# First query step moved beside the last key tiles, and the start of the next pair's attention reordered, in a convolution, attention and routed-MLP kernel

## What is computed

```python
x = x + conv(_gn(x), ...)      # x: (16, 64, 56, 56) f32; conv below
t = to_tokens(x)               # 3136 tokens of 64 features for each image
t = t + attention(_ln_t(t))    # 16 heads of 64, features elu + 1, linear attention
t = t + routed_mlp(_ln_t(t))   # 32 experts, each takes its 8 best tokens
x = from_tokens(t)

# conv: t3[a,k,b] = sum over pixels of x shifted by 2k-6 columns times x
#       t12 = 5x5 dilated depthwise(x) - (7-tap product with t3 - 1x5 depthwise(t2)), t2 = 1x3 conv(x)
# attention: q, k = elu(proj) + 1; positions enter as cos and sin
qkv   = q_cos @ (k_cos.T @ v) + q_sin @ (k_sin.T @ v)
denom = 1 / (q_cos . sum(k_cos) + q_sin . sum(k_sin) + 1e-5)
out   = (qkv * denom) @ dense_w.T + dense_b
```

## Time and profile before

| | |
|---|---|
| median of 3 runs | 3526.32 us (3520.82 to 3526.87) |
| the profiled execution: time, span | 3529.31 us, 3527.5 us |
| PE busy in the span | 3191.5 us (90%) |
| DVE, ACT, POOL busy | 2415.9, 1975.6, 1968.3 us |
| granted TensorE clock, mean | 0.982 |
| one pair in the loop | about 415 us |

### The profile page before, as it was taken

The page is one execution under the profiler, slowest core; times in us unless marked ns, Lnnn a source line. Parts: engine busy times, 40 slices in busy tenths (PEclk is TensorE's granted clock), DMA queues, the critical chain, the costliest instruction groups (busy, mean ns, idle before and its releaser), DMA issues.

```text
span 3527.5 us, 44913 instructions
## 1 busy us (share of the span) xinstructions
PE 3191.5 (90%) x17092; PEld 1488.6 (42%) x17092; DVE 2415.9 (68%) x2773; ACT 1975.6 (56%) x2209; POOL 1968.3 (56%) x1303
## 2 busy tenths in 40 slices
PE   3898999989899998989989898998989999899977
PEld 2543345434443335433454344443354333543333
DVE  5887766967668676776668666686756866645754
ACT  1166654766556764666646665476645676444430
POOL 1167861878428882478727785297833888121320
PEclk8999999999999999999999999999999999999988
DMA  2002740046300661016510363005620075202678
GB/s 55 19 1 57 156 104 28 1 98 146 82 19 0 145 143 56 1 29 152 133 31 0 80 152 85 28 1 125 141 60 19 2 161 135 52 1 65 149 169 279
DMA packets 69297, 278.75 MB, mean 79 GB/s; under 512 B 30845, under 2 KB 35485, under 8 KB 64221
## 3 DMA queue, kind: packets, MB, share of 16 engines
q1 hardware_dynamic: 69085, 275.89, 32.5%
HBM read 242.78 MB, written 33.05 MB: 78 GB/s over the span
## 4 chain that ended last, share of the span: by engine, by line
PE 72%; DVE 11%; ACT 7%; DMA 5%; issue 4%; SPq 1%; POOL 0%; DVEq 0%; ACTq 0%; POOLq 0%
PE ps_D L1590 15%; PE ps_C L1523 10%; PE ps_A L1508 5%; PE ps_B L1508 5%; PE ps_D L1523 5%; PE ps_E L1568 5%; PE ps_E L1523 5%; PE ps_B L1552 3%; PE ps_D L1366 3%; PE ps_A L1552 3%; DVE region L1149 2%; PE ps_A L1385 2%; DMA RB<-r_keep 2%; DVE arena L1000 2%; DMA r_keep<-RR 2%
## 5 line engine op out<-in xcount | busy, mean ns | idle before, releaser
L610 POOL TENSOR_TENSOR arena<-arena,UHL 128x896 f32<-128x896 f32 x525 | 1106.6, 2112 | 252.8 <-ACT UHL L771 252.6
L1590 PE MATMUL ps_D<-region,small 128*128 128x448 f32 x1792 | 759.3, 550 | 9.7 <-DVE OS L1185 6.6
L592 POOL TENSOR_TENSOR region<-region,RB 128x896 f32<-128x896 f32 x224 | 468.9, 2093 | 174.9 <-DMA RB<-r_keep 174.5
L771 ACT ACTIVATE UHL<-arena,W8C 128x896 f32<-128x896 f32 x525 | 540.9, 1033 | 0.4
L620 POOL TENSOR_TENSOR UA<-region,CS 128x128 f32<-128x128 f32 (+1 forms) x400 | 224.6, 563 | 449.4 <-PE ps_C L1523 401.3
L1590 PEld LDWEIGHTS ps_D<-region,small 128*128 128x128 f32 x1792 | 322.9, 190 | 291.8 <-issue 237.8
L815 ACT ACTIVATE EQ<-ps_B,NEG 128x896 f32<-128x896 f32 x224 | 225.5, 1007 | 361.4 <-PE ps_B L1552 361.4
L1523 PE MATMUL ps_C<-region,UA 128*128 128x512 f32 (+1 forms) x800 | 382.5, 601 | 18.1 <-ACT region L689 18.1
L1000 DVE SCALAR_TENSOR_TENSOR arena<-arena,W8C 128x448 f32<-128x448 f32 (+1 forms) x235 | 358.3, 1545 | 0.0
L1158 DVE TENSOR_TENSOR region<-region,ps_C 128x896 f32<-128x896 f32 x224 | 242.9, 1084 | 142.3 <-ACT ps_C L779 142.0
L1125 DVE SCALAR_TENSOR_TENSOR region<-region,ps_A 128x1024 f32<-128x1024 f32 (+1 forms) x200 | 242.6, 1213 | 140.2 <-ACT region L797 140.2
(11 more groups left out here) (308 smaller groups left out, 4983.8 us busy)
## 6 DMA issues: line engine op xcount, KB each, us to landing
RB<-r_keep SPq DMA_DIRECT2D x448, 448.0 KB, 6.0
arena<-x SPq DMA_DIRECT2D x8, 1568.0 KB, 6.6
t_keep<-Y SPq DMA_DIRECT2D x7, 1568.0 KB, 5.2
r_keep<-RR SPq DMA_DIRECT2D x448, 7.0 KB, 2.9
w_keep<-region SPq DMA_DIRECT2D x7, 784.0 KB, 5.5
arena<-w_keep SPq DMA_DIRECT2D x4, 784.0 KB, 10.6
arena<-L_ffn_weight SPq DMA_DIRECT2D x1, 2080.0 KB
CST<-cst SPq DMA_DIRECT2D x1, 1568.0 KB, 6.4
```

What stands on the lines that cost most here:

```text
L592: pool.tensor_tensor(out=q, in0=q, in1=RB[:, cc].rearrange("p (c n) -> p c n", c=2), op=ALU.mult).then_inc(pool_scaled.sem, 1)
L610: pool.tensor_tensor(out=X[:, cut], in0=X[:, cut], in1=PRODUCT[m % 3], op=ALU.add).then_inc(pool_taps.sem, 1)
L771: act.activation(PRODUCT[m % 3].rearrange("p (h w) -> p h w", w=W), g_window(2 * g * ROWS + 2 * (k // 5), 2 * (k % 5) - 4, 2 * ROWS), ACT. ...
L1590: ins = pe.matmul(here.area(key)[:, 0:PIX], MW[i][:, c, :], Q[s % 3][:, c, :], start=c == 0, stop=c == NCHUNK - 1)
```

## The change

It renumbers the work around two seams of a pair.

At the seam of key tiles and query slots, step 0 of the queries leaves the slots. The first image's head matrices stand beside key tiles 29 and 31, its four projections beside tiles 33, 35, 37 and 39, its denominators beside 41 and its sums beside 43, all through ps_C, one at a time. Its features lie in un2 and SQ (`features`). DVE's pieces leave tiles 30, 32, ... 42 and 43 (`NO_PIECE`), so that 23 of the 25 are done beside the tiles, up to the last one, and two in slots 12 and 15. The first projection of step 1 stands before the last key product. The slots begin with step 1 and are 66 in number; the second image's head matrices stand in slots 1 and 3, the four outputs of step 0 in slots 2, 4, 6 and 8. Chunks 0 and 2 of step 0 are multiplied by DVE straight from RB in SBUF (`first_scale`), without ACT's copy to PSUM. Tap products fill four of five slots, before three of four.

At the seam of back and key tiles, the turned correlation waits for its copy only (`t3_copied`), `conv(0)` for the turned taps only from its fifth tap, the routing weights are turned before `conv(2)` into ps_A, ps_D and ps_E, group 0 is split before group 1 is turned, and `conv(3)` is last. Group 1 is scaled beside tile 0 and split beside tile 2, and POOL's deviations of group 1 stand before its first UA. Group 3 goes through ps_D beside tile 2.

```diff
-YT_TILES = [None, None, 0, 1]
-SUM_TILES = [None, None, 1, 2]
+YT_TILES, YT_AREAS = [None, None, 0, 2], "__CD"
+SUM_TILES = [None, None, 1, 3]
-SCALE_TILES = [None, None, 8, 12]
-SPLIT_TILES = [None, 0, 9, 13]
-UTS_TILES = [None, 2, 12, 18]
+SCALE_TILES = [None, 0, 8, 12]
+SPLIT_TILES = [None, 2, 9, 13]
+UTS_TILES = [None, 4, 12, 18]
+WT_GROUPS = [(0, 16), (16, 8), (24, 1)]
-PRODUCT_TILE, PRODUCT_SLOT, POOL_LAG, DRAIN_SLOT = 20, 3, 4, 64
+HEAD_TILES, FIRST_TILES, FIRST_DEN, FIRST_SUM = (29, 31), (33, 35, 37, 39), 41, 43
+NO_PIECE = (30, 32, 34, 36, 38, 40, 42, 43)
+PRODUCT_TILE, PRODUCT_SLOT, POOL_LAG, PIECE_SLOT, DRAIN_SLOT = 20, 1, 1, 12, 60
-PRODUCT_SLOTS = {PRODUCT_SLOT + n + n // 3: n for n in range(POOL_PIECES - TILE_PRODUCTS)}
-SLOTS = 4 * STEPS
+PRODUCT_SLOTS = {PRODUCT_SLOT + n + n // 4: n for n in range(POOL_PIECES - TILE_PRODUCTS)}
+SLOTS = 4 * (STEPS - 1)
+HEAD_SLOTS = (1, 3)
+FIRST_OUT_SLOTS = {2: 0, 4: 1, 6: 2, 8: 3}
+FIRST_POOL_SLOTS, FIRST_PARTS_SLOT = {0: 1, 2: 3}, 10
-ALL_SLOTS = 70
+ALL_SLOTS = 66
...
+                uses += [(("m", 0, HEAD_TILES.index(k)), "C")] if k in HEAD_TILES else []
+                uses += [(("qp", 0, FIRST_TILES.index(k)), "C")] if k in FIRST_TILES else []
+                uses += [(("den", 0), "C")] if k == FIRST_DEN else []
+                uses += [(("dsum", 0), "C")] if k == FIRST_SUM else []
...
+            def first_scale(here, cc):
+                q = features(0, cc)
+                dve.wait_ge(*spread_loaded[cc // 2].at(here.pair, 1))
+                dve.tensor_tensor(out=q, in0=q, in1=RB[:, cc].rearrange("p (c n) -> p c n", c=2),
+                                  op=ALU.mult).then_inc(first_scaled.sem, 1)
...
                 norm_sums(squared(0), ln1_sums, 0)
                 norm1_scale(here, pair, 0)
-                norm_sums(squared(1), ln1_sums, 1)
                 low_part(pair, 0)
                 conv_residual(here, pair, 2)
-                norm1_scale(here, pair, 1)
+                norm_sums(squared(1), ln1_sums, 1)
                 conv_residual(here, pair, 3)
...
-                    if conv and k > NORM_TILE:
-                        depthwise(here, pair + 1, K_PIECES, DVE_PIECES)
-                for i in range(2):
-                    head_matrices(here, i)
+                    if k - 1 in HEAD_TILES:
+                        head_matrices(here, 0, HEAD_TILES.index(k - 1))
+                    if k - 1 in FIRST_TILES:
+                        q_features(here, 0, FIRST_TILES.index(k - 1))
+                    if k == FIRST_DEN + 1:
+                        den_parts(here, 0)
+                    if k == FIRST_SUM:
+                        den_guard(here, 0)
+                        den_reciprocal(here, 0)
+                    if conv and k > NORM_TILE and k not in NO_PIECE:
+                        depthwise(here, pair + 1, 1, DVE_PIECES)
+                first_scale(here, 0)
...
             def turned_correlations(here):
-                pe.wait_ge(*here.emptied("t3"))
+                pe.wait_ge(*(t3_copied.first(1) if here.span == "setup" else t3_copied.at(here.pair, 1)))
...
                 turned_correlations(here)
                 conv(here, 0)
                 conv(here, 1)
-                for g in (0, 1):
-                    pe.wait_ge(*here.emptied(("conv", g)))
-                    to_tokens(here, 1, g)
-                    if g == 0:
-                        conv(here, 2)
+                pe.wait_ge(*here.emptied(("conv", 0)))
+                to_tokens(here, 1, 0)
                 routing_weights(here)
+                conv(here, 2)
                 pool_tokens(here)
+                split_tokens(here, pair, 0)
+                pe.wait_ge(*here.emptied(("conv", 1)))
+                to_tokens(here, 1, 1)
+                pool_turned(here)
                 conv(here, 3)
-                pool_turned(here)
-                split_tokens(here, pair, 0)
```

More of the change, by code:

```diff
@@ L95, in slot_of_step, with step_of, chunk_of @@
 def slot_of_step(j, lag):
-    return j >= lag and (j - lag) % 4 == 0 and (j - lag) // 4 < STEPS
+    return j >= lag and (j - lag) % 4 == 0 and (j - lag) // 4 < STEPS - 1
+def step_of(j):
+    return j // 4 + 1
+def chunk_of(j):
+    return j // 4 + 1, j % 4
 def copied_slot(j):
@@ L270, in pair_uses @@
             uses += [(("lg", g), misc()) for g in range(NG)]
-            return uses + ([(("wt", g), misc()) for g in range(2)] + [("pool", "D"), ("pool_turned", "E")] if last
+            return uses + ([(("wt", g), "ADE"[g]) for g in range(3)] + [("pool", "D"), ("pool_turned", "E")] if last
                            else back_uses())
@@ L676, in tokens @@
                     act.wait_ge(*square_free)
+                if which == 2 and g == 0:
+                    act.wait_ge(*here.filled(("out", 0)))
                 src = here.area(key)[:, 0:m * P].rearrange("p (t c) -> p t c", c=P)
@@ L789, in products_out, with q_exponential @@
                         .then_inc(*here.empty(key))
+            def q_exponential(here, s, cc):
+                key = ("qp", s, cc)
+                act.wait_ge(*here.filled(key))
+                act.activation(EQ[:, cc % 2], here.area(key)[:, :].rearrange("p (c n) -> p c n", c=2)[:, :, 0:PIX],
+                               ACT.Exp, bias=NEG1[:, 0:1]).then_inc(eq_ready.sem, 1)
             def pair_of_images(here):
@@ L1145, in q_features @@
                 dve.wait_ge(*eq_ready.at(here.pair, n + 1))
-                if s >= 3:
+                if s == 1 and cc == 0:
+                    dve.wait_ge(*ua_ready.at(here.pair, KTILES))
+                if s >= 4:
                     dve.wait_ge(*(here.filled(("out", s - 3)) if cc == 3
@@ L1262, in _ @@
                 now[0] = lambda n: vstep.at(pair, n)
-                pair_of_images(Here("loop", pair))
+                pair_of_images(Here("loop", pair), Here("loop", pair - 1) if pair else start)
                 assert links[0] == VLOOP, links[0]
@@ L1266, in _ @@
             now[0] = lambda n: vstep.at(PAIRS - 1, n)
-            pair_of_images(Here("last", PAIRS - 1))
+            pair_of_images(Here("last", PAIRS - 1), Here("loop", PAIRS - 2))
             end = Here("final")
@@ L1402, in conv @@
                 if g == 0:
-                    pe.wait_ge(*here.emptied("t3t"))
+                    pe.wait_ge(*here.emptied("t3"))
                     for w in here.all_emptied([("t2", m) for m in range(NG)]):
@@ L1406, in conv @@
                 for k in range(7):
+                    if g == 0 and k == 4:
+                        pe.wait_ge(*here.emptied("t3t"))
                     ins = quarters(here, g, L10[:, k, :],
@@ L1587, in q_output @@
                 pe.wait_ge(*(scaled_by_pool(here.pair, s, cc) if cc in POOL_SCALED
-                             else here.emptied(("rb", s, cc))))
+                             else here.emptied(("rb", s, cc)) if s else first_scaled.at(here.pair, cc // 2 + 1)))
                 for c in (2 * cc, 2 * cc + 1):
-                    ins = pe.matmul(here.area(key)[:, 0:PIX], MW[i][:, c, :], Q[s % 3][:, c, :],
+                    ins = pe.matmul(here.area(key)[:, 0:PIX], MW[i][:, c, :], features(s, cc)[:, c % 2, :],
                                     start=c == 0, stop=c == NCHUNK - 1)
@@ L1618, in pair_of_images @@
                         k_products(here, k - 2)
+                    if k == FIRST_DEN:
+                        for g in range(2):
+                            q_denominators(here, 0, g)
                     if k in UTS_TILES:
@@ L1732, in _ @@
                         .then_inc(*end.fill(key))
-VSETUP = 44
-VLOOP = 12
+VSETUP = 42
+VLOOP = 11
 LOW = -3.0e38
```

237 lines of the change are left out of this document (132 added, 105 removed).

## The result

| | median | lowest to highest | runs |
|---|---|---|---|
| before | 3526.60 us | 3520.82 to 3534.48 | 4 |
| after | 3484.81 us | 3483.41 to 3488.96 | 4 |

The ratio is 0.9882, 95% interval 0.9861 to 0.9903: the change makes the kernel faster by 42 us, half of the 83.5 that were forecast, and the time lies above the range of 3405 to 3480. The profiled execution has a span of 3487.2 us at a mean granted clock of 0.975.

What follows compares the result with a forecast made beforehand. PE was taken to bound the kernel, with only its idle 30 us a pair to win. First seam 28 plus second seam 55.5 made 83.5 us off 3529.3, 3445.8, about 3443 as median; 80% range 3405 to 3480.

Steps and rivals of the forecast that it cites:

- What bounds the kernel, and where the idle lies: PE is busy 384.7 of 415 us a pair; of its idle, 10.9 us lie at the first seam, 8.6 at the second.
- Second seam, 55.5 us: From correlation's end to the fourth key product: idle nearly all gone, 7.5 us in seven pairs and 3 in the first.
- the 0.8 kept back: Second seam: 0.8 us a pair taken off the walked 8.3 us, for hops between engines.
- The 3 us of the first pair: Second seam of the first pair: 3 us won, since its first tiles show the same two waits.
- Key tiles, 11.0 us: First seam: key tiles end about 11.0 us later, 7.8 work moved in, 6.1 waits, 0.7 hops, less 3.4 slack.
- The rival that all seven hand-overs cost 2.6 us: Key tiles: every ps_C hand-over costs 2.6 us, 18.2 us of waits instead of 6.1; slower than before, 3540; 4%.
- Slots, "comes to the first output of step 1 27.4 us after": Query slots: first output of step 1 comes 27.4 us after the end of the key tiles, by walking both queues.
- the price of `first_scale` at 1.95 us: Start of the slots: each DVE multiplication from RB takes 1.95 us, the 1949 ns row measured where POOL runs.
- the gain of 15.0: Slots: first output of step 1 comes 27.4 instead of 42.4 us after the key tiles, winning 15.0 us a pair.
- first seam gives nothing: Rival: new waits at the ps_C hand-overs use up the first seam's 28 us; 3471 us; 13%.
- What the changed profile would show: PE busy nearly unchanged, span 75 to 90 us shorter, `first_scale` 1.6 to 2.1 us, ps_C waits of 2.6 and 0.8.
- The three signs named for a wrong forecast: ps_C waits above 2 us each, DVE's first slots late for RB, or the first key product waiting for POOL.

Runs made afterwards that it cites:

- s2: The kernel before with only the second-seam part of the change, query step 0 left in the slots; 3459.94 us, ratio to before 0.9802.
- e1: The changed kernel with POOL's two scalings of step 0 moved from slots 0 and 2 to slots 3 and 5; 3432.80 us, ratio to before 0.9724.
- e2: The changed kernel without DVE's piece behind key tile 49, made up later; 3472.89 us, ratio to before 0.9837.
- e3: The changed kernel with the two `first_scale` operations beside key tiles 48 and 49, in place of the pieces there; 3483.66 us, ratio to before 0.9873.
- e5: e1 with five DVE reductions of a constant, read by nobody, ahead of the first `first_scale` in each pair; 3480.29 us, ratio to before 0.9851.

## Why the prediction was wrong

- **What bounds the kernel, and where the idle lies**: right.
- **Second seam, 55.5 us**: the mechanism is right and the size too small, 69. The walk gave 8.3 us a pair, and that is what the pair it started from shows (54.2 to 46.0), so the 0.8 kept back was not needed. The term left out is the clock: in the other six pairs the waits that went away were followed by 1.6 to 4.9 us of slower matmuls (55.8 to 59.1 before). That the walk's pair was the one without them was bad luck, and one look at another pair would have shown it. The 3 us of the first pair did not come: its last UA on POOL begins at 300.71 us in s2 and at 298.99 before.
- **Key tiles, 11.0 us**: measured 11.7, with waits of 5.8 for 6.1. The rival that all seven hand-overs cost 2.6 us is refuted; the largest is 1.8.
- **Slots, "comes to the first output of step 1 27.4 us after"**: this is the step that failed, and in it the price of `first_scale` at 1.95 us with the piece ahead of it at about 1.7. They take 2.96 and 5.82. The 1949 ns are a mean of operations of 2.3 us, each let in behind the one POOL operation that it met, and of 1.08 us with POOL at rest (2.31, 2.29 and 1.08 in the pair of the earlier trace rows). I took it as the price and never looked at what POOL's own queue does at slot 0, although the diff puts two scalings there and the text says that RB lies ready. Against the 6.9 us missing stand 5.1 from the piece (5.82 - 1.74) and `first_scale` (2.96 - 1.95), 2.0 from the clock behind the wait (7.4 us at 0.70, most of it busy), and about 1 from a second slow stretch right before that output, which e1 has in five of its pairs (27.3 against 25.9). The second `first_scale`, 1.08 for 1.95, gives up to 0.9 back. With the row broken up (e1) the stretch is 25.5 to 27.4 us: the walk itself was good.
- **What was new and where it was read**: 42.4 us for the old stretch came from one pair. The eight have 39.7 to 43.9, 41.7 in the mean (41.1 from 1135.74 to 1176.84, for one), so the gain of 15.0 was 0.7 too large.
- **The range**: the rival "first seam gives nothing" stopped at 0. Measured it costs 22 to 25 us. The page "SBUF — State Buffer" of the Trainium skill, section "Who interferes with whom", on the shared port pair, was cited for the right place, and read as if one DVE operation met one of POOL's. The rule that the two exclude one another holds here. Its length does not: by the rule the loser waits for one operation, and the piece waited for three.
- **What the changed profile would show**: PE busy 3186.3 us for 3191.5, waits into ps_C of 1.8 and 0.9, and no key product waiting for ACT came as told; the span is 40 shorter and not 75 to 90, and `first_scale` at 2.96 and 1.08 lies on both sides of the 1.6 to 2.1. The three signs named for a wrong forecast all stayed away: the one that failed it was not on the list.
- **The sum**: 83.5 + 13.5 (second seam) - 53 (first seam, -25 for +28) = 44; measured 41.8. The 2 us between them are the difference of the two medians of before (3528.97 and 3526.60).

## What to carry to other kernels

Where a transfer or a wait is removed ahead of an engine's operations, ask what that engine will now run back to back, and whose operations it can hold meanwhile: here two GpSimd operations that had become ready early cost more than the step that they belong to gained. Delaying work that nobody waits for is worth as much as hastening work that somebody does (two numbers in a table gave 52 us), and so is the order of two ready operations on an engine (45 us). And a price from a by-form mean holds only where the neighbours do what they do on average; an operation that decides a walk needs its own row, at its own place.

## What the runs showed of the hardware

- A DVE operation with two SBUF operands that is issued while POOL runs a row of such operations without a gap can wait for several of them: a 0.68-us piece took 5.82 us behind three of a row of four, 3.77 behind two of a row of two; a 1.08-us multiplication took 6.29 behind three and 8.31 behind four. Where the row of four let DVE in after the third, POOL's last one took 2.45 us instead of 2.08.
- This is no rule for every such row. In the slots of the change eleven pieces are issued in a tap sum that a scaling follows without a gap, and each is let in after the tap sum:

```profile
1585.83 1.69 DVE L1043 SCALAR_TENSOR_TENSOR arena<-arena,W8C 128x448 f32<-128x448 f32 x1
...
1587.00 2.48 POOL L627 TENSOR_TENSOR region<-region,RB 128x896 f32<-128x896 f32 x1
```

  What decides whether DVE gets in between two POOL operations stays open, and with it why the row of four let it in after the third in the change and in e2, and not in e3 or in the change's fifth pair.
- Between the tap sums of the key tiles stands a UA, also without a gap, and there a piece takes 1.74 us only: it gets in behind one tap sum. The UA takes 0.40 us where no piece is beside it, 0.78 where one is, and 1.25 in e3 where it is `first_scale` (1.08 us alone). So the UA waits for DVE, and does not run beside it.
- Reductions with one SBUF operand were not held: the five of e5 took 5.04 us, 1.07 each, two of them beside a tap sum.
- A wait of 5.2 to 5.8 us was followed by a granted clock below 1.00 in every pair that had one: 0.71 to 0.77 over the 7 us right behind it in the change, 0.57 to 0.77 in e5. Shorter waits are less regular: behind the 2.3 us before the first key product before, the clock over 7 us was 0.76 in five of the eight pairs and 1.00 in three.
